# Cross attention on one Trainium2 core: scores as float32r pairs of heads in PE's rows, and the scores of a block ahead of its values and small steps

## What is computed

```python
hd = DIM // HEADS                                  # 256 // 16 = 16
q = (x @ Wq).reshape(B, N, HEADS, hd).transpose(0, 2, 1, 3)
k = (context @ Wk).reshape(B, M, HEADS, hd).transpose(0, 2, 1, 3)
v = (context @ Wv).reshape(B, M, HEADS, hd).transpose(0, 2, 1, 3)
scores = jnp.einsum('bhid,bhjd->bhij', q, k) * hd ** (-0.5)
scores = jnp.where(context_mask[:, None, None, :], scores, max_neg)
attn = jax.nn.softmax(scores, axis=-1)
out = jnp.einsum('bhij,bhjd->bhid', attn, v)
return out.transpose(0, 2, 1, 3).reshape(B, N, DIM) @ Wo
```

## Time and profile before

| what | before |
|---|---|
| median of 3 runs | 1218.95 us (1217.62 to 1220.98) |
| span of the profiled execution | 1218.4 us |
| PE busy over the span | 1139.0 us (93%) |
| DVE busy | 954.2 us (78%) |
| ACT busy | 612.3 us (50%) |
| POOL busy | 371.0 us (30%) |

### The profile page before, as it was taken

One profiled execution on the slowest core, in us unless ns is written; L12 is line 12 of the kernel. 1 busy time (PEld: TensorE's weight loads), 2 busy tenths in 40 slices (PEclk: granted clock), 3 DMA queues, 4 the chain that ended last, 5 costly groups with the idle time before them and its releaser, 6 DMA issues. The chain is left out here.

```text
span 1218.4 us, 29643 instructions
## 1 busy us (share of the span) xinstructions
PE 1139.0 (93%) x11668; PEld 685.0 (56%) x11669; DVE 954.2 (78%) x1745; ACT 612.3 (50%) x1166; POOL 371.0 (30%) x351
## 2 busy tenths in 40 slices
PE   7899899999999999879999999999999847999996
PEld 6566666676677777643443344334434334676665
DVE  5989968987888688788778778877889466677757
ACT  4332333334333333227777767777788722344443
POOL 2422255222522222113200320221100424556651
PEclk9899999999999999999999999999999978999999
DMA  7100026000400000025720580075050152121125
GB/s 242 48 1 2 2 51 111 2 2 1 82 1 2 1 2 2 1 59 83 151 35 9 105 157 2 8 141 95 2 212 2 53 139 93 61 65 61 63 60 210
DMA packets 62200, 73.64 MB, mean 60 GB/s; under 512 B 14352, under 2 KB 53392, under 8 KB 61440
## 3 DMA queue, kind: packets, MB, share of 16 engines
q1 hardware_dynamic: 58288, 61.56, 21.3%
q0 software_dynamic: 3792, 10.36, 2.8%
HBM read 52.86 MB, written 18.78 MB: 59 GB/s over the span
## 5 line engine op out<-in xcount | busy, mean ns | idle before, releaser
L1737 DVE TENSOR_REDUCE neg_max<-pS 128x1 f32<-128x1024 f32 x238 | 285.0, 1220 | 50.9 <-PE pS L1520 50.8
L1652 ACT ACTIVATE pt<-pR 128x512 f32<-128x512 f32 x512 | 286.3, 600 | 73.4 <-PE pR L1543 68.5
L1543 PE MATMUL pR<-qs,ks 100*32 100x512 bf16 x2048 | 192.4, 381 | 1.9 <-ACT pt L1652 1.6
L1520 PE MATMUL pS<-ks,qs 100*32 100x512 bf16 x1904 | 146.4, 378 | 3.4 <-DVE neg_max L1737 1.8
L1557 PE MATMUL b_pO<-pt,b_v 128*32 128x512 f32 x1024 | 135.0, 598 | 3.0 <-ACT pt L1652 2.3
L411 PE MATMUL pP<-w_feat,a_xT 128*128 128x512 f32 x244 | 116.4, 600 | 0.7 <-ACT w_feat L689 0.7
L1543 PEld LDWEIGHTS pR<-qs,ks 100*32 100x32 bf16 x2048 | 57.2, 96 | 93.7 <-issue 23.8
L301 POOL TENSOR_TENSOR kf<-kf,fsum 128x2048 f32<-128x2048 f32 (+1 forms) x17 | 58.1, 3420 | 163.8 <-DVE fsum L883 163.8
L301 POOL TENSOR_TENSOR qs<-qs,fsum 128x2048 f32<-128x2048 f32 (+1 forms) x17 | 58.5, 3446 | 141.2 <-DVE fsum L883 141.2
L716 ACT COPY qfT<-pT 128x512 f32<-128x512 f32 x64 | 37.2, 582 | 126.3 <-PE pT L439 126.3
L1399 POOL COPY qs<-max_rows 3x512 bf16<-3x512 bf16 x60 | 36.7, 611 | 210.1 <-ACT max_rows L1645 207.1
(11 more groups left out here) (353 smaller groups left out, 2145.0 us busy)
## 6 DMA issues: line engine op xcount, KB each, us to landing
ks<-k_scr SPq DMA_DIRECT2D x8, 768.0 KB
qs<-q_scr SPq DMA_DIRECT2D x24, 256.0 KB
k_scr<-f SPq DMA_DIRECT2D x18, 256.0 KB, 2.7
ks<-k_scr SPq DMA_DIRECT2D x8, 512.0 KB
ks<-in_L_ffn_w_dram SPq DMA_DIRECT2D x2, 2048.0 KB, 10.5
ks<-in_L_ffn_w_dram SPq DMA_DIRECT2D x4, 1024.0 KB, 9.2
ks<-y_rows SPq DMA_DIRECT2D x16, 256.0 KB, 5.3
cx<-in_ctx_dram SPq DMA_DIRECT2D x3, 768.0 KB, 12.4
```

The lines of the kernel that those rows point to most:

```text
L1520: ins = pe.matmul(pS1[q:q + XV, slot, 512 * half:512 * half + 512], qs[0:KR, bass.ds(par, 1), h, P * t + q:P * t + q + XV].rearrange("r a ...
L1543: ins = pe.matmul(ring[bank][q:q + XV, :], ks[0:KR, bass.ds(par, 1), h, P * j + q:P * j + q + XV].rearrange("r a n -> r (a n)"), qs[0:KR, ...
L1652: nc.scalar.activation(pt[:, j % 2, i, :], ring[bank], ACT.Exp).then_inc(exp_done, 1)
L1737: nc.vector.tensor_reduce(neg_max[:, hg % 2, u // G, u % G:u % G + 1], pS1[:, u % 2, :], AX_X, ALU.max, negate=True).then_inc(max_done, 1)
```

## The change

- The stacks become float32r (the 4-byte type of PE's operands that is shorter than fp32). Each query or key is two parts, `parts[..., 0]` the value written as float32r and `parts[..., 1]` the rest. Three products of parts are summed, in 3 x 16 rows with the four extra ones between: `KR` = 52.
- Two heads stand side by side in the partitions, the even one from 0, the odd one from 64 (`HALF`). Each score product now has 128 columns of weights and works on rows 0 to 51 or 64 to 115. A unit is two heads x 512 positions (`unit_of`), so a row's maximum comes in two halves, which `split_max` joins with one more operation (`ALU.min` of the negated ones).
- In a block `scores_by_context` does heads 0 and 1, then a unit, then heads 2 and 3, then a unit; then come the values of the block before, then all small steps (`early` returns 0). ACT and DVE follow this order.
- POOL no longer splits; ACT writes the first part and DVE the second. The semaphore `s2_done` becomes two, for even and odd heads.
- `k_scr`, `q_scr` and `aug_scr` are float32, loads go by parity of heads (`rows_by_parity`), and `xn` moves into `v_new`.

```diff
+F32R = mybir.dt.float32r
-PAIRS = ((0, 0), (0, 1), (0, 2), (1, 0), (1, 1), (2, 0))
-K_RUNS = ((0, 3), (3, 2), (5, 1))
-AUG = XD * len(PAIRS)
-KR = AUG + 4
+AUG, AUG_END = 2 * XD, 2 * XD + 4
+KR = AUG_END + XD
+K_ROWS = ((0, 0, 2), (AUG_END, 0, 1))
+Q_ROWS = ((0, 0), (XD, 0), (AUG_END, 1))
+def rows_by_parity(parts, e):
+    return parts.rearrange("c (d h two) n -> two (c d) h n", d=XD, two=2)[e]
+def max_home(q_rows, par, head):
+    at = HALF * (head % 2) + AUG
+    return q_rows[at:at + 3, par, head // 2, :]
+def unit_of(u):
+    return u // 4, u % 4 // 2, u % 2
...
         def early(steps):
-            return len(steps) if steps and steps[-1][0] == "m_turn" else max(len(steps) - 1, 0)
+            return 0
...
                 def scores_by_token(b, hg, u):
...
-                    for half in range(2):
-                        for q in range(0, P, XV):
-                            ins = pe.matmul(
-                                pS1[q:q + XV, slot, 512 * half:512 * half + 512],
-                                qs[0:KR, bass.ds(par, 1), h, P * t + q:P * t + q + XV].rearrange("r a n -> r (a n)"),
-                                ks[0:KR, bass.ds(par, 1), h, 512 * half:512 * half + 512
-                                   ].rearrange("r a n -> r (a n)"), start=True, stop=True)
+                    for e in range(2):
+                        at = HALF * e
+                        ins = pe.matmul(pS1[:, u % 2, 512 * e:512 * e + 512],
+                                        qs_r[at:at + KR, b % 2, 2 * hg + pair, P * t:P * t + P],
+                                        ks_r[at:at + KR, b % 2, 2 * hg + pair, 512 * half:512 * half + 512],
+                                        start=True, stop=True)
...
-                def scores_by_context(b, hg, j, i, bank):
-                    if j == 0:
-                        wait(pe, m_copied, G * (G * b + hg - 1) + i + 1)
-                    par, h = b % 2, G * hg + i
-                    for q in range(0, P, XV):
-                        ins = pe.matmul(ring[bank][q:q + XV, :],
-                                        ks[0:KR, bass.ds(par, 1), h, P * j + q:P * j + q + XV
-                                           ].rearrange("r a n -> r (a n)"),
-                                        qs[0:KR, bass.ds(par, 1), h, :].rearrange("r a n -> r (a n)"),
-                                        start=True, stop=True)
-                    ins.then_inc(s2_done, 1)
+                def scores_by_context(b, start, hg, j, pair, banks, ahead_of):
+                    for i in (2 * pair, 2 * pair + 1):
+                        bank_is_read(b, start, ahead_of["score", hg, j, i])
+                        if j == 0:
+                            wait(pe, m_copied, G * (G * b + hg - 1) + i + 1)
+                        at = HALF * (i % 2)
+                        ins = pe.matmul(ring[banks["score", hg, j, i]],
+                                        ks_r[at:at + KR, b % 2, 2 * hg + pair, P * j:P * j + P],
+                                        qs_r[at:at + KR, b % 2, 2 * hg + pair, :], start=True, stop=True)
+                        ins.then_inc(s2_done[i % 2], 1)
...
-                            for i in range(2):
-                                bank_is_read(b, start, ahead_of["score", hg, j, i])
-                                scores_by_context(b, hg, j, i, banks["score", hg, j, i])
-                                if i == 0:
-                                    for ahead, g, u in units[:1]:
-                                        scores_by_token(b + ahead, g, u)
+                            scores_by_context(b, start, hg, j, 0, banks, ahead_of)
+                            for ahead, g, u in units[:1]:
+                                scores_by_token(b + ahead, g, u)
+                            scores_by_context(b, start, hg, j, 1, banks, ahead_of)
+                            for ahead, g, u in units[1:]:
+                                scores_by_token(b + ahead, g, u)
                             values_before(b, hg, j, first)
...
-                            for i in range(2, G):
-                                bank_is_read(b, start, ahead_of["score", hg, j, i])
-                                scores_by_context(b, hg, j, i, banks["score", hg, j, i])
-                                if i == 2:
-                                    for ahead, g, u in units[1:]:
-                                        scores_by_token(b + ahead, g, u)
...
-                        nc.vector.scalar_tensor_tensor(rest[:, :], pM[:, :], q_scale[:, bass.ds(b, 1)],
-                                                           head, ALU.mult, ALU.subtract).then_inc(emptied, 1)
...
                 def split_max(b, hg, own, steps):
...
-                    nm = neg_max[:, hg % 2]
-                    own.did(nc.vector.tensor_copy(max_parts[:, :, :, 0], nm))
+                    own.did(nc.vector.tensor_tensor(max_now[:, :, :], neg_max[:, hg % 2, 0], neg_max[:, hg % 2, 1],
+                                                    ALU.min))
                     own.wait()
+                    own.did(nc.vector.tensor_copy(max_parts[:, :, :, 0], max_now[:, :, :]))
```

More of the change, by code:

```diff
@@ L276, in _ @@
+                sp.wait_ge(first_loaded, LOADED)
             @block.gpsimd
@@ L1250, in ring_user_ahead, with done_by @@
             return ahead
-        def cT_by(first):
+        def done_by(first, step):
             order = [step for g in range(G) for j in range(JT) for step in small_steps(g, j, first, False)]
-            return order.index(("cT", 3)) + 1
+            return order.index(step) + 1
         FIRST, MIDDLE = steps_of(True, False), steps_of(False, False)
@@ L1283, in load_cx, with load_k @@
                     sp.dma_start(cx[:, :, :], ctx_in[b].rearrange("(j p) c -> p j c", p=P)).then_inc(s_cx, 16)
-                def load_k(b, half, heads, done):
+                def load_k(b, half):
                     now = slice(512 * half, 512 * half + 512)
-                    for at, n in K_RUNS:
-                        sp.dma_start(ks[XD * at:XD * (at + n), b % 2, heads, now],
-                                     k_scr[b, 0:n].rearrange("c (d h) n -> (c d) h n", d=XD)[:, heads, now]).then_inc(done, 16)
@@ L1291, in load_k_aug @@
-                def load_k_aug(b, heads, done):
-                    sp.dma_start(ks[AUG:KR, b % 2, heads],
-                                 aug_scr[b].unsqueeze(1).broadcast_to([4, heads.stop - heads.start, M])
-                                 ).then_inc(done, 16)
-                def load_q(b, heads, done):
-                    for s, pair in enumerate(PAIRS):
-                        sp.dma_start(qs[XD * s:XD * s + XD, b % 2, heads],
-                                     q_scr[b, pair[0]].rearrange("(d h) n -> d h n", d=XD)[:, heads]).then_inc(done, 16)
@@ L1301, in load_q_aug @@
-                def load_q_aug(b, heads, done):
-                    sp.dma_start(qs[AUG:KR, b % 2, heads],
-                                 q_aug[AUG:KR, :].unsqueeze(1).broadcast_to([4, heads.stop - heads.start, L])
-                                 ).then_inc(done, 16)
+                    for e in range(2):
+                        for at, c, n in K_ROWS:
+                            sp.dma_start(ks_r[HALF * e + at:HALF * e + at + XD * n, b % 2, :, now].bitcast(F32),
+                                         rows_by_parity(k_scr[b, c:c + n], e)[:, :, now]).then_inc(k_loaded, 16)
@@ L1306, in store_k, with load_q_aug @@
+                def load_q_aug(b):
+                    for e in range(2):
+                        sp.dma_start(qs_r[HALF * e + AUG:HALF * e + AUG_END, b % 2].bitcast(F32),
+                                     q_aug[AUG:AUG_END, :].unsqueeze(1).broadcast_to([4, XH // 2, L])
+                                     ).then_inc(q_loaded, 16)
                 def store_k(b, half):
                     n = entry(b, "k", 2 * half)
-                    wait(sp, split_done, 2 * (n + 1))
-                    for c in range(3):
+                    wait(sp, emptied, prepared(b, ("k", 2 * half + 1)))
+                    for c in range(2):
@@ L1318, in store_q @@
-                    for c in range(3):
+                    wait(sp, emptied, prepared(b, ("q", 1)))
+                    for c in range(2):
                         sp.dma_start(q_scr[b, c].rearrange("(m p) n -> p m n", p=P),
-                                     parts[:, n % 2, c]).then_inc(stored[2], 16)
-                    wait(sp, stored[2], 48 * b)
+                                     parts[:, n % 2, c].bitcast(F32)).then_inc(stored[2], 16)
+                    wait(sp, stored[2], 32 * b)
```

261 lines of the change are left out of this document (133 added, 128 removed).

## The result

The change made the kernel slower: 1264.9 us (median of 4 runs, 1263.2 to 1270.6) against 1218.7 us (1217.6 to 1221.0), a ratio of 1.039 with a 95% interval of 1.036 to 1.042. The profiled execution has a span of 1263.1 us, 44.7 over that of before; the sum of the forecast was 28. The time lies in the stated range (1222 to 1285 us) but above the forecast case (1237 to 1258).

A forecast was written before the change was run, and what follows sets the result against it. PE was taken to bound cross attention. Batches added 6.6, 8.1 twice and 4.0 us, together 26.8, with linear attention 28; 1218.4 + 28 = 1246.4, plus 0.6 for the median over the span, 1247 us; range 1222 to 1285 us.

The forecast's parts named there:

- forecast case: Whole kernel, all terms of the sum holding: 1247 us, around 1237 to 1258 by the drain; chance 62%.
- rival of pairs in turn: In cross attention the two products of a pair run one after the other: about 32 us, 1279 us; chance 12%.
- The drain: On PE, changing between row-tile scores and column-tile values and back costs 0.25 us in each of 128 blocks, 32 us.
- The fourth score waits for the first exponential: Three-bank ring: 1.15 us from first pair to fourth score, PE standing 0.50; a plain block 2.70 us against 2.62.
- forecast sign: In cross attention, PE 0.5 us idle before every fourth score, released by ACT's exponential.
- The small steps: Moved to the end of a block, they add 1.1, 2.5 and 2.3 us in a middle batch.
- double blocks: Three blocks of a middle batch with two steps, the second waiting for the first: about 0.77 us each, 2.3 us.
- Behind k and q steps: Next block's third score waits while ACT and DVE read the step's bank: about 0.42 us, 6 per batch, 2.5 us.
- copy ahead of the first exponential: A step's copy on ACT makes the next block's first exponential 0.14 us later, about 8 blocks per middle batch, 1.1 us.
- Half rate or four passes: Float32r scores on PE: half rate, pair and unit 0.43 us each, 1312 us, 10%; four passes, about 1465 us, 3%.
- Faster because columns count: Before the fourth score, exponential and hand-overs take under 0.65 us, so DVE would bound: about 1150 us; chance 6%.
- No drain: On PE, changing between row and column tiles is free, so the 32 us go: +5, 1224 us; chance 7%.

The follow-up runs named there:

- e12: The kernel before with a small extra product ahead of every third score, one wide in the second batch, four narrow in the third; 1230.4 us.
- e7: The changed kernel with exponentials of 256 of the 512 queries from the third block on; 1241.6 us.
- e5: The changed kernel with the values back between second and third score, small steps still last; 1241.4 us.
- e4: The changed kernel without ACT's wait on the values before a block's first exponential; 1264.4 us.
- e6: The changed kernel with the first of two small steps and the turn of the maxima back between second and third score; 1258.2 us.
- e9: The changed kernel, its order kept, with every score product reading the even head in rows 0 to 51; 1333.0 us.
- e1: The changed kernel's products with each block in the order of the kernel before; 1216.4 us.
- e3: The changed kernel with a block's values as one fp32 product in rows 0 to 63, head 0 alone; 1307.3 us in fast runs.
- e10: The changed kernel's products, all in rows 0 to 51, in the order of the kernel before; 1294.4 us.

## Why the prediction was right, and where its sum was off

The direction and the mechanism were right: PE's freed time is lost in front of the fourth score, and the drains and steps make the change slower. The size was not. The measured 1264.9 us lie above the forecast case (1237 to 1258), between it and the rival of pairs in turn (1279), in a stretch that the range covers only because it was drawn wide enough for that rival. That the time fell into the range is in part luck: the steps, priced too high, hid nearly half of what the plain blocks were priced too low.

**PE bounds cross attention; PE's column time is not what counts.** Right. The pair takes 0.22 us as taken, 110 us of columns went, and the stage grew by 43.

**The drain, 0.25 us per block.** Nearly right: 0.11 from unit to values (in a plain block of the second batch 776.624 to 776.947, less a pass of 0.22), 0.11 from values to the next record (777.401 to 777.943, less the 0.43 of the second four), and 0.20 for both in e12.

**The fourth score waits for the first exponential.** Right in kind (e7 moves the block one to one, e5 shows the cover that was lost), but mis-sized: the term "plain block 2.70 us" measured 2.90. I had 0.44 us to the exponential, from a bf16 block where the weight loads were hidden, and one load of 0.06 from transposes. After a change of arrangement, and after a wait, the float32r load stands in the open with 0.10 (record 0.497, and 0.393 where it is hidden), twice a block: ahead of the pair and ahead of the fourth score. And ACT's second wait is an instruction of its own, 0.06 us (e4). So 1.25 for 1.15 up to the fourth score, 0.65 for 0.56 from there to the values: 0.2 us, 128 times, 26 us more than the sum had. This is the step that failed. (The forecast sign, PE idle for 0.5 us before every fourth score, did not come as said: a record lasts longer than its stream, and the plain block above shows 0.28.)

**The small steps.** Too dear, which hid nearly half of that error. For a middle batch the sum had 5.9 us beyond the plain blocks; measured are 12.0 - 32 x 0.28 = 3.0. The double blocks gave 0.70, 0.50 and 0.97 beyond the 0.28, 2.2 us, as forecast (2.3; e6 takes 2.5 off them and 2.2 off the batch). Behind k and q steps it was 0.28 to 0.39 in four blocks, 1.3 us for 2.5; that a longer plain block gives the readers more time fits this and was not tested. The copy ahead of the first exponential (1.1 us) cost nothing that shows in the sum. e4 fits that: behind such a copy, taking the wait instruction away gains nothing, as if the copy stood in its place. In the first and last batch the steps came out at -0.3 and -0.6 us.

**The rest.** Linear attention +1.1 for 1. Loads, POOL's splits and the extra operation on the maxima: nothing seen. About 2 us at the lower clock in the third batch, and whatever the 6.8 us of it in the first cost, were not forecast. Together: plain blocks 36 us for 9, steps and clock 7 for 18, 43.2 for 26.8.

**Rivals.** Pairs in turn: no, though with them in turn the block would indeed grow by 0.23 (e9). Half rate or four passes: no, 0.22 per product of 512 columns. Faster because columns count: no, exponential and hand-overs took 1.25 us, not under 0.65. No drain: no, 0.11 each way. e1's expectation has a slip of its own: six streams, values, drains and one or two loads are 2.51 to 2.61 us, not 2.4 to 2.5, and the blocks measured 2.41 to 2.72.

## What to carry to other kernels

Before freeing an engine's time, write down for each wait on a buffer what work covers it; here PE's products became four times fewer, and the same reordering took away the cover of a 1.25 us round trip per block. Cost such a chain from records that have the new operands' exposed parts (a weight load behind a wait or a change of arrangement, a second wait as an instruction), not from a block where they are hidden: 0.2 us, 128 times, was over half of this result. And try an edit's two halves apart: the products alone were worth -4 us, the order alone +33, and together +46.

## What was not expected of the hardware

- Products of the two row halves pass one another on PE: 706.307 for one that stands in the program behind the one of 706.637 (e1), and so in 220 of its 238 units. The Trainium skill (TensorE: Matmul & The Clock Gate, Step-by-step: what each phase is for) says that "the MATMULs themselves stay in program order"; for their start the trace says otherwise when they use different rows. The fp32 values in one half that start beside a unit's product in the other (e3) use the same freedom without overtaking.
- The granted clock fell to the 1.2 GHz level in the middle of PE's work: for 3.4 us in the third batch of the changed kernel (PE's records cover 6.9 of the 8 us before), for most of the second batch in e3 (mean 0.60; from 706.2 to 818.9 it stayed there with PE busy for 110.7 of 112.7 us), in e9's first batch (0.83), while e1's second batch, with PE busy for 110.7 of 111.7 us, had 1.00. What sets it is open. The kind of product alone does not: e10 has e9's products in another order, and its second batch had 1.00.
